# Taking the filler matmuls out of four norms and two single-expert layers of a fused graph-and-attention network

## The reference

```
# block 0, graph network: three rounds of message passing
for l in range(3):
    agg = segment_sum(nodes[src] + nodes[dst] + edge_proj, dst)
    h = concatenate([nodes, agg]) @ W1[l].T + b1[l]
    h = relu(layernorm(h, ln_g[l], ln_b[l]))          # the norm "lnh"
    nodes = h @ W2[l].T + b2[l] + nodes

# block 1: the attention with random features ends in a norm of its own
y = x + x_attn @ W_proj + b_proj
y = layernorm(y) * gamma + beta                       # the norm "lny"

# blocks 0 and 2, feed-forward with one expert of eight for each node
probs = softmax(xt @ Ws + bs)
routes, prob_max = argmax(probs), max(probs)
h = act(xt @ W1[e] + b1[e]); y = h @ W2[e] + b2[e]    # e = the node's route
out = y[routes] * prob_max                            # "moe0", "moe2"
```

## Time and profile before

| | before |
|---|---|
| three timed runs | 4636.38, 4647.54, 4648.42 us; median 4647.54 us |
| the profiled execution, its own time | 4637.39 us |
| its span, first to last instruction | 4635.4 us |
| PE busy in the span | 95% |
| DVE, ACT | 22%, 22% |
| mean granted clock of PE | 0.983 |

### The profile page before, as it was taken

How to read it: one execution, slowest core, us unless ns; L and a number is a source line. 1 busy time by engine, 2 the same in 40 slices (tenths; PEclk the granted TensorE clock), 3 DMA queues, 4 the chain that set the end, 5 groups by cost and what they waited for, 6 DMA issues and landing times.

```text
span 4635.4 us, 38002 instructions
## 1 busy us (share of the span) xinstructions
PE 4417.1 (95%) x15188; PEld 1979.0 (43%) x15213; DVE 1018.0 (22%) x1894; ACT 1008.2 (22%) x1830; POOL 90.1 (2%) x169
## 2 busy tenths in 40 slices
PE   8999999999999997989999999999899999999998
PEld 3444444444445543444444444443444334334333
DVE  6872011212311226123300000022532000000000
ACT  3122112324213326222210101012722011111000
POOL 1000000000000000000000000000000000000000
PEclk9999999999999998989999999999899999999999
DMA  9512222121372120113203031256127999999998
GB/s 322 159 69 87 77 68 81 55 73 55 116 307 64 46 82 0 46 37 103 69 23 102 25 100 36 87 192 253 37 73 323 416 423 423 411 423 414 424 415 352
DMA packets 128786, 795.71 MB, mean 172 GB/s; under 512 B 13950, under 2 KB 26542, under 8 KB 82172
## 3 DMA queue, kind: packets, MB, share of 16 engines
q1 hardware_dynamic: 116892, 728.07, 41.6%
q0 software_dynamic: 9280, 45.81, 2.6%
q10 hardware_dynamic: 2464, 19.67, 1.1%
HBM read 774.47 MB, written 56.83 MB: 179 GB/s over the span
## 4 chain that ended last, share of the span: by engine, by line
PE 87%; DMA 5%; DVE 4%; ACT 3%; issue 1%; POOL 0%; SPq 0%; ACTq 0%; DVEq 0%; POOLq 0%
PE bank L531 78%; DMA mem<-in_experts 4%; PE bank L678 4%; PE bank L529 3%; PE bank L652 2%; DVE mem L2367 1%; DVE mem L2363 0%; ACT mem L1690 0%; ACT mem L1711 0%; ACT mem L1852 0%; DVE mem L2032 0%; ACT mem L1348 0%; ACT mem L1726 0%; DVE rstd L2013 0%; DMA mem<-y_by_slot,slot_i 0%
## 5 line engine op out<-in xcount | busy, mean ns | idle before, releaser
L531 PE MATMUL bank<-mem 128*128 128x512 f32 (+5 forms) x11160 | 3530.1, 556 | 57.7 <-DMA mem<-in_experts 25.4
L531 PEld LDWEIGHTS bank<-mem 128*128 128x128 f32 (+3 forms) x11160 | 1480.8, 167 | 2025.5 <-issue 1894.6
L529 PE MATMUL bank<-ident,mem 128*128 128x128 f32 (+2 forms) x1484 | 223.0, 301 | 86.9 <-issue 24.1
L529 PEld LDWEIGHTS bank<-ident,mem 128*128 128x128 f32 (+2 forms) x1484 | 187.5, 155 | 175.3 <-issue 99.6
L1348 ACT ACTIVATE mem<-bank 128x512 f32<-128x512 f32 x171 | 101.8, 597 | 544.0 <-PE bank L531 539.2
L1348 ACT ACTIVATE mem<-bank,cols 128x512 f32<-128x512 f32 (+1 forms) x88 | 60.4, 686 | 713.9 <-PE bank L531 713.9
L531 PE MATMUL bank<-mem,ones 128*128 128x512 f32 (+1 forms) x380 | 170.0, 614 | 24.4 <-ACT mem L1382 15.9
L678 PE MATMUL bank<-mem 128*128 128x512 bf16 x799 | 175.9, 379 | 0.9 <-issue 0.2
L2661 DVE TENSOR_TENSOR mem<-mem,EV 128x512 f32<-128x512 f32 x48 | 33.2, 693 | 552.7 <-ACT EV L1950 552.7
L2639 DVE TENSOR_TENSOR mem<-mem,bank 128x512 f32<-128x512 f32 x48 | 33.0, 688 | 453.3 <-PE bank L531 453.3
L678 PEld LDWEIGHTS bank<-mem 128*128 128x128 bf16 x816 | 79.3, 98 | 97.4 <-DVE mem L2142 1.3
(11 more groups left out here) (361 smaller groups left out, 2093.3 us busy)
## 6 DMA issues: line engine op xcount, KB each, us to landing
mem<-in_experts SPq DMA_DIRECT2D x282, 1536.0 KB, 11.9
mem<-in_weights SPq DMA_DIRECT2D x329, 512.0 KB, 3.5
mem<-moe_up SPq DMA_DIRECT2D x30, 1152.0 KB, 9.1
mem<-moe_down SPq DMA_DIRECT2D x30, 1152.0 KB, 10.2
moe_up<-in_weights SPq DMA_DIRECT2D x16, 1152.0 KB
moe_down<-in_weights SPq DMA_DIRECT2D x16, 1152.0 KB
mem<-in_weights POOLq DMA_DIRECT2D x36, 384.0 KB, 7.5
mem<-in_experts ACTq DMA_DIRECT2D x6, 1536.0 KB, 14.7
```

The source lines that it names most:

```text
L529: ins = nc.tensor.transpose(out, lhsT, ident[0:lhsT.shape[0], 0:lhsT.shape[0]])
L531: ins = nc.tensor.matmul(out, lhsT, rhs, start=start, stop=stop)
```

## The change

The three constants and the three loops that issue fillers go. That is 5 products in each of the three rounds of `lnh` and in `lny`, and 13 + 9 in each of the two single-expert layers: 64 products, 128 instructions of PE. No other instruction, wait or DMA changes, and the order of what is left is the same.

```diff
@@ -36,7 +36,6 @@
-FILL_ROUTE, FILL_BACK = 13, 9
@@ -54,7 +53,6 @@
-FILL = 5
@@ -620,8 +618,6 @@ norm_sums
                 square_sums(label)
-                for k in range(FILL if label in ("lnh", "lny") else 0):
-                    mm(bank[5][:, :], ones[:, :], sq[:, k, :])
@@ -880,8 +876,6 @@ experts_of_one
                 ins.then_inc(agg_done.sem, agg_done.tick((tag, "ranks")))

-                for n in range(FILL_ROUTE):
-                    mm(bank[6][:, :], ones[:, :], XT[:, 0, :])
                 slots_t(0)
                 up(0)
@@ -894,8 +888,6 @@ experts_of_one
-                for n in range(FILL_BACK):
-                    mm(bank[4][:, :], ones[:, :], XT[:, 0, :])
                 for t in range(NT):
                     scaled = act_done if t >= 2 else dve_done
                     pe.wait_ge(scaled.sem, scaled.at((tag, "scaled", t)))
```

## The result

The changed kernel took 4655.47 us (median of 12 runs, 4646.21 to 4668.52), the kernel before, run beside it, 4641.75 us (12 runs, 4633.59 to 4648.42). The ratio is 1.0029, with a 95% interval of 1.0020 to 1.0038: 13.5 us slower (9.3 to 17.6), at the edge of the 0.3% that was called no change. The time lies in the stated range; the forecast was +4.3 us. So the size was off by a factor of three, and two terms of the sum were wrong. The twelve times of before also fill the gap between the "two pairs" of the prediction: all of them are one spread, of which the prediction had seen four.

The account below looks back on a forecast made before the run. PE, busy 95% of a 4635.4 us span, was taken to bound the kernel; -4.28 (lny) + 7.2 (lnh) + 0.8 (routing) + 0.6 (way back) = +4.3 us, ratio 1.0009, predicted 4652 us, range 4637 to 4661.

Parts of the forecast that it names:

- two pairs: Timed runs of the kernel before were taken as a lower and an upper pair of times, 10 us apart.
- lnh, +7.2: Three lnh rounds: 5.89 us of idleness drops PE to half clock, losing 2.4 us each; bounds 4.8 to 10.2.
- lny, -4.28: At lny the fillers lie in PE's way, so the linear layer starts 4.28 us earlier; bounds 3.6 to 4.3.
- Nothing is late in its place: At lny, nothing the earlier linear layer needs holds it up, so the 4.28 us gain is kept.
- Routing, +0.8 with a bound of 3.4: Two routings: 2.1 us more at half speed, partly covered, costing 0.4 us each; bounds 0 and 1.7 each.
- second rival: Half speed outlasts its cause, chiefly 10 us at each routing: +19.3 us, 4667, slower by over 0.3%; chance 0.05.
- the cover by waits for weights: In the expert stage, PE's loss at the start shortens later weight waits; 1.0 us taken as 0.4 per routing.
- Way back, +0.6: Two ways back: transposes at half speed, mostly covered by waiting for DVE; 0.3 us each, bounds 0 and 1.7.
- first rival: The clock doesn't bite: lnh stays at full speed and only lny counts, -2.9 us, 4644.6; chance 0.14.
- the third: Rival: fillers at the norms kept nothing warm and were pure cost; faster by over 0.3%, chance 0.02.

Follow-up runs that it names:

- e1: Kernel before with only the fillers of the three lnh rounds out; ratio 1.0015, +7.0 us.
- e2: Kernel before with only the fillers of lny out; ratio 1.0001, +0.5 us.
- e5: Kernel before without lny's fillers, and with ACT emptying four banks before the logarithm of the counts; ratio 0.9989, 5.1 us faster.
- e10: Kernel before with all fillers kept, only ACT's order changed: four banks emptied before the logarithm of the counts; ratio 1.0004, 1.9 us slower.
- e3: Kernel before with only the 13 products at the routing out, in both single-expert layers; ratio 1.0016, +7.4 us.
- e6: Kernel before with 6 products instead of 13 at the routing, all other fillers in place; ratio 1.0009, 4.2 us slower.
- e11: Kernel before with the 13 routing products out and 5 full-width ones issued after the slots arrive; 4661.04 us against 4642.91.
- e4: Kernel before with only the 9 products on the way back out, in both single-expert layers; ratio 1.0003, +1.4 us.
- e8: e5's edits plus fillers at the softmax attention, two graph networks and proj3, against the kernel before; ratio 0.9993, 3.2 us faster.
- e9: e8 without the graph-network fillers, with 14 and 15 routing products instead of 13, against the kernel before; ratio 0.9968, median 4628.94 us.

## Why the prediction came out as it did

**lnh, +7.2: right.** 7.0 us by e1 (2.8 to 11.1), 2.1 to 2.8 us lost a round in the changed kernel and 1.6 to 2.7 in e1, against 2.4 forecast. That PE would be idle 5.89 us, start at the same place, and not be covered was seen as forecast.

**lny, -4.28: wrong.** The step that failed is the sentence "Nothing is late in its place". It checked the weight ring and ACT's root, but not what stands behind the root in ACT's queue. The linear layer needs a free bank from its fifth output on, and ACT frees none before the logarithm of the counts. In the kernel before, with the fillers ahead of it, PE finished its fourth output at 1622.28 + 20.6 = 1642.9, about 1.3 us after ACT had begun to free banks (1641.56). So no wait showed in its trace, and a layer that starts 4.3 us earlier had to run into one. Measured +0.5 us (-3.7 to +4.6), in place of a gain: in e2 the layer even ended 0.9 us later behind the root, 36.0 us against 35.1. e5 and e10 show that both holds had to go.

**Routing, +0.8 with a bound of 3.4: wrong in size.** Measured +7.4 (3.3 to 11.6) by e3. I assumed that the half speed would end where it ended before, and only begin earlier. It was the row of before, 3.3 us at half, that misled: there PE entered the expert stage at full speed after full-width fillers. Entering at half speed, the narrow first work takes 8 to 9 us to bring the clock back (the changed kernel, e3, e6), where full-width work took 4.6 to 5.6 (e11). The second rival named this mechanism, with 10 us for each routing, and argued against it from that same row. And the cover by waits for weights, which I used to halve the term, did not show in e3: moe0 lost the 2.8 us and moe2 the 4.2 that half of the added half-speed work gives. In the changed kernel moe2 lost 1.8 us against before, within what that stretch varies by itself.

**Way back, +0.6: right in mechanism, the size not resolved.** +1.4 (-2.8 to +5.6) by e4, nothing in the stretches of moe0, 0.3 and 0.8 us in those of moe2.

**The sum.** 7.2 - 4.3 + 0.8 + 0.6 = 4.3 became 7.0 + 0.5 + 7.4 + 1.4 = 16.3 by single edits, 13.5 as a whole. The range held because its top was built from bounds and from the spread of four timed runs; the part of it from the supposed two pairs of times was not sound. With two terms too low by 4.8 and 6.6 us in the same direction, that the total stayed inside was partly luck. The first rival (the clock doesn't bite) and the third (pure cost) fell.

## What to carry to other kernels

A filler that lies in a wait can be worth more than it seems: here those at lnh and the routing were worth about 2 to 4 us at each place. Judge it by what PE does next: in this kernel narrow products and transposes brought the clock back slowly, so the fillers ahead of them were worth most, and had to reach up to the wait (half of them saved 1.3 us of 7.0 by the stretches). Then look at the next fall of the clock as well, which may grow and take part of the gain back. When something is taken out ahead of an engine, follow each resource that it will now reach earlier, the output banks above all, to the engine that frees it and through all of that engine's queue. And a hold without a wait in the trace may be a second hold hidden behind the first.

## What was not expected of the hardware

After 12.6 to 13.9 us of idleness PE stayed at 1.2 GHz through 8.0 to 9.1 us of transposes, two-row and half-width products, but through only 4.6 to 5.6 us of full-width products, at the same place and after the same idleness. With 7.1 and 8.7 us of idleness it was 9.1 and 8.0 us of work again. And once fillers had removed a fall, the next one, some 95 or 50 us later, lasted 6.8 us instead of 3.4 (e8, e9, two places). And 3.3 us of idleness cost lnh as much (6.4 us in three rounds) as 5.9 us (7.0 to 7.5).

By the Trainium skill ("TensorE: Matmul & The Clock Gate", Part 4) a transpose does not count as busy in the way a product does. The traces agree in part: in e11 full-width products brought the clock back sooner than work that begins with transposes, but what share the transposes have in that, no run here shows. Transposes can run at full speed: 24 of them did so in the kernel before, in 2.83 us.
